# Second layer in a different cyclic order, its start written out, its first buffers loaded during the experts

## What is computed

```
x = x + L0_xattn(layernorm(x), ctx)     # 16 heads
x = x + L0_ffn(layernorm(x))            # routing to 8 experts, 512 places each, token kept or sent
x = x + L1_xattn(layernorm(x), ctx)     # 16 heads, then relu(out @ W1 + b1) @ W2 + b2
x = x + L1_ffn(layernorm(x))            # the cell below, then a layernorm
```

```
for c in range(6):
    q = ew[c,0]*(nodes[in_q] @ We[eq] + be[eq])      # k, v likewise, from other nodes and edges
    nodes[c] = act_w[c]*mha(q, k, v, Wq[c], Wk[c], Wv[c], Wo[c]) + q
```

## Time and profile before

| | |
|---|---|
| profiled execution | 4160.97 us, of which the span of the trace is 4159.2 us |
| median of the three timed runs | 4163.48 us |
| PE busy | 4031.4 us (97% of the span) |
| ACT, DVE, POOL busy | 2628.5 (63%), 2472.9 (59%), 1932.9 (46%) |
| first layer, experts, second layer | 0 to 654, 658 to 897, 897 to 4159 us |
| DMA | mean 31 GB/s over the span |

### The profile page before, as it was taken

The page is one execution under the profiler, slowest core; times in us unless marked ns, Lnnn a source line. Parts: engine busy times, 40 slices in busy tenths (PEclk is TensorE's granted clock), DMA queues, the critical chain, the costliest instruction groups (busy, mean ns, idle before and its releaser), DMA issues.

```text
span 4159.2 us, 100757 instructions
## 1 busy us (share of the span) xinstructions
PE 4031.4 (97%) x38276; PEld 3405.7 (82%) x38276; DVE 2472.9 (59%) x6184; ACT 2628.5 (63%) x11786; POOL 1932.9 (46%) x2011
## 2 busy tenths in 40 slices
PE   7999998988999999999999999999999999999997
PEld 6888876666888888888888888888888888888885
DVE  5777772024566666666666666666666666666553
ACT  6888871214666666666666666666666666666664
POOL 6888982113444444444444444444444444444332
PEclk9999999999999999999999999999999999999999
DMA  3232214430000000000000000000000000000000
GB/s 102 70 98 72 70 45 140 132 116 23 12 14 14 14 17 21 13 14 14 13 13 16 13 13 13 12 12 12 12 12 12 12 20 12 12 12 12 7 4 6
DMA packets 117867, 129.75 MB, mean 31 GB/s; under 512 B 12006, under 2 KB 110676, under 8 KB 117264
## 3 DMA queue, kind: packets, MB, share of 16 engines
q1 hardware_dynamic: 101664, 106.26, 8.0%
q0 software_dynamic: 6144, 8.43, 0.7%
q10 hardware_dynamic: 9584, 8.61, 0.7%
HBM read 89.68 MB, written 41.94 MB: 32 GB/s over the span
## 4 chain that ended last, share of the span: by engine, by line
PE 75%; DVE 1%; ACT 1%; DMA 0%; POOL 0%; issue 0%; ACTq 0%; POOLq 0%; SPq 0%; DVEq 0%
PE c_product L1374 35%; PE c_product L1385 15%; PE c_product L1433 10%; PE c_scores L1423 7%; PE c_product L1456 5%; PE c_product L1444 2%; ACT c_probs L1187 1%; DVE c_qT L1233 1%; PE c_product L1362 1%; PE c_product L1493 0%; DVE c_neg_max L1242 0%; DMA c_probsT<-in_L_ffn_Wk 0%; ACT c_front_probs L1187 0%; POOL c_probs L1135 0%; DMA c_probsT<-in_L_ffn_Wv 0%
## 5 line engine op out<-in xcount | busy, mean ns | idle before, releaser
L1135 POOL TENSOR_TENSOR c_probs<-c_probs,c_row_inv 128x512 f32<-128x512 f32 x768 | 794.2, 1044 | 1525.8 <-DVE c_row_inv L1245 1525.1
L1187 ACT ACTIVATE c_probs<-c_scores,c_neg_max 128x128 f32<-128x128 f32 x3072 | 1086.6, 409 | 606.1 <-DVE c_neg_max L1242 606.1
L1374 PE MATMUL c_product<-c_nodes,cell_w 128*128 128x256 f32 x4352 | 1064.2, 384 | 6.1 <-DVE c_nodes L1233 3.9
L1374 PEld LDWEIGHTS c_product<-c_nodes,cell_w 128*128 128x128 f32 x4352 | 802.6, 190 | 133.1 <-DVE c_nodes L1233 12.8
L1187 ACT ACTIVATION_READ_ACCUMULATOR c_probs<-c_scores,c_neg_max 128x1 f32 x3072 | 762.1, 248 | 0.0
L1242 DVE TENSOR_REDUCE c_neg_max<-c_scores 128x4 f32<-128x512 f32 x1024 | 635.6, 683 | 179.7 <-PE c_scores L1423 179.5
L1193 ACT COPY c_probsT<-c_product 128x512 f32<-128x512 f32 x768 | 416.2, 611 | 237.8 <-PE c_product L1433 235.0
L1187 ACT ACTIVATE c_front_probs<-c_scores,c_neg_max 128x128 f32<-128x128 f32 x1024 | 359.0, 401 | 149.0 <-DVE c_neg_max L1242 149.0
L1385 PE MATMUL c_product<-cell_w,c_nodes 128*128 128x256 f32 x1792 | 432.7, 381 | 1.6 <-DVE c_kT L1233 1.6
L1433 PE MATMUL c_product<-consts_sb,c_probs 128*128 128x128 f32 x3072 | 403.1, 275 | 15.2 <-POOL c_probs L1135 15.0
L420 ACT ACTIVATE a_probs<-a_scores,a_neg_max 128x128 f32<-128x128 f32 x1024 | 361.9, 399 | 82.3 <-DVE a_neg_max L476 81.7
(11 more groups left out here) (167 smaller groups left out, 6679.4 us busy)
## 6 DMA issues: line engine op xcount, KB each, us to landing
e_w<-in_L_ffn_w SPq DMA_DIRECT2D x12, 1024.0 KB, 6.5
a_x<-in_x SPq DMA_DIRECT2D x32, 256.0 KB, 2.9
a_ctxT<-in_ctx_pairsT SPq DMA_DIRECT2D x32, 256.0 KB, 3.1
x<-a_x SPq DMA_DIRECT2D x32, 256.0 KB, 2.2
xn<-a_xn SPq DMA_DIRECT2D x32, 256.0 KB, 2.1
c_routed<-xn SPq DMA_DIRECT2D x32, 256.0 KB, 2.9
c_x<-x SPq DMA_DIRECT2D x32, 256.0 KB, 3.2
c_ctxT<-in_ctx_pairsT SPq DMA_DIRECT2D x32, 256.0 KB, 2.8
```

The source lines that it names most:

```text
L1135: nc.gpsimd.tensor_tensor(e, e, rinv[:, i, r].unsqueeze(2).broadcast_to([P, 4, T]), ALU.mult).then_inc(norm_made, 1)
L1187: a = nc.scalar.activation(probs(n)[:, r, k], S[r][:, k], ACT.Exp, bias=nmax[:, i, r, k:k + 1], accum_out=rsum[:, i, r, k:k + 1])
L1374: i = T_.matmul(m[:, u], w[:, k, u * P:(u + 1) * P], src[:, k], start=n == 0, stop=n == last)
```

## The change

Four edits are made in one.

1. The four order tables are replaced by others. PE's new period has the pairs A2 S0, S3 A5, A0 f.Sb0, A3 S1, A4 S2 and the three A1 f.Sb1 f.Ab0 directly behind one another (A0 f.Sb0 and A4 S2 stood so before). The front part of a job now begins one period earlier (offset -1).
2. The first pieces of each engine are written out in PE_HEAD (99 pieces), DVE_HEAD, ACT_HEAD and POOL_HEAD, with F and B pieces among them; `headed` puts the table ahead and takes its pieces out of the unfolded order.
3. The weights and biases of the second layer, the four ring buffers' first contents and job 0's rows and context are loaded by SP in the experts' block, at experts 4 to 7. Their memory is given out before the experts' phase. The routed rows of expert 0 are waited for by SP before it loads w2 of expert 0.
4. f.Ab0 and f.Ab1 write a buffer of their own (`front_oT`) instead of sharing xT; the stores of finished jobs are issued five jobs later instead of three (STORES_BEHIND), ahead of the context load; POOL zeroes vE and vO behind its first gather.

```
 PE_ORDER = """
-S3:2 T0.1:1 f.Tx:0 f.K:0 V3:2 f.Q:0 A0:1 f.Sb0:0 K1:1 O0:1 T3.0:2 K4:2 T3.1:2 Q1:1 A3:2 f.Tb0.0:0 S1:1
...
+O4:2 f.Ab1:0 Q5:2 f.W1a:0 f.W1b:0 f.Tx:-1 f.W2:0 T2.0:1 S5:2 T2.1:1 V2:1 f.Q:-1 f.Txn:0 V5:2 Q0:0 K0:0 A2:1
...
+def headed(table, order):
+    head = [(t.rpartition(":")[0], int(t.rpartition(":")[2])) for t in table.split()]
+    return head + [x for x in order if x not in head]
...
+            sp.wait_ge(rows_in[0], 16)
             sp.dma_start(w2t[:, 0], tiles(w2[0])).then_inc(w2_in[0], 16)
...
+                if e == 4:
+                    for n, a in (("wk", "L1_xattn_Wk_rows"), ("wq", "L1_xattn_Wq"), ("wv", "L1_xattn_Wv_rows"),
+                                 ("w1", "L1_xattn_W1"), ("w2", "L1_xattn_W2")):
+                        sp.dma_start(early[n][:], tiles(io[a])).then_inc(early[n + "_in"], 16)
...
+                if e == 6:
+                    for n in range(FUSED_FIRST, FUSED_FIRST + len(early["late"])):
+                        fuse_load(sp, io, fused, n, early)
+                if e == E - 1:
+                    sp.dma_start(early["routed"][:], rows_of(scratch["xn1"], 0)).then_inc(early["rows0_in"], 16)
+                    sp.dma_start(early["x"][:, 0], rows_of(scratch["x1"], 0)).then_inc(early["x0_in"], 16)
+                    sp.dma_start(early["ctxT"][:], tiles(io["ctx_pairsT"][0])).then_inc(early["ctx0_in"], 16)
...
-        oF = xT
+        oF = sb("front_oT", [2, W2])
...
-            late_load(act, FUSED_FIRST)
...
             for j in range(2, JOBS):
                 load_rows(j)
+                if j >= STORES_BEHIND:
+                    store(j - STORES_BEHIND)
                 load_context(j)
-                if j >= JOBS_IN_FLIGHT:
-                    store(j - JOBS_IN_FLIGHT)
```

More of the change, by code:

```diff
@@ L895 @@
+S4.e1:1 S4.e2:1 S4.e3:1 f.Tb0^2:-1
 """
 POOL_ORDER = """
[L898 to L910 removed]
@@ L911 @@
-f.Tb0.0:0 B14
-f.Ab0:0 F15 F16 B15
-f.Tb1.0:0 B16 F17
-f.Tb1.1:0 B17
-"""
-LATE_FUSE_DVE_PLACES = """
-start:0 F6^ B6^ F7^
-f.x2:0 B7^
-f.st:0 F8^ B8^
-f.x:0 F9^ B9^ F10^
-f.Tx^:0 B10^
-f.Q^:0 F11^
-f.x2:1 B11^
-f.Sb0.i1:0 F12^
-f.Sb0.i3:0 B12^ F13^ B13^
-f.x:1 F14^ B14^
-f.Sb1.i0:0 F15^
-f.Ab0^:0 F16^
-f.Sb1.i2:0 B15^
-f.Sb1.i3:0 B16^ F17^ B17^
-"""
-def phase_second_layer(nc, io, scratch, keep, cell, cst, out):
+S5.n3:3 S0.n2:1 S0.n3:1 S3.n0:2 S3.n1:2 f.ga:-1 S3.n2:2 f.Sb0.n0:0 S3.n3:2 f.Sb0.n1:0 S1.n2:1 S1.n0:1 S1.n1:1
@@ new lines @@
+f.Tb0.0:1 Q1:0 B15:0 S1:0 K2:0 V1:0 K3:0 f.Tb0.1:1 f.Sb1:1 T1.0:0 T1.1:0 F17:0 A1:0 f.Ab0:1 O1:0 f.Tb1.0:1
+f.Tb1.1:1 Q2:0 f.Ab1:1 S2:0 f.W1a:1 f.W1b:1 f.Tx:2 f.W2:1 V2:0 B16:0 T2.0:0 f.K:2 f.Txn:1 K0:1 Q0:1 T2.1:0
+S0:1 A2:0 O2:0 B17:0 Q3:0 T0.0:1 S3:0 V3:0 f.Q:2 V0:1 T0.1:1 K1:1 f.Sb0:2 A0:1 T3.0:0 O0:1 T3.1:0
+"""
+ACT_HEAD = """
+f.Sb0.e0:0 f.Sb0.e2:0 f.Sb0.e1:0 f.Sb0.e3:0 f.Tb0^1:0 f.Tb0^0:0 f.Tb0^3:0 f.Tb0^2:0 f.Sb1.e2:0 f.Sb1.e0:0
+f.Sb1.e1:0 f.Sb1.e3:0 f.Tb1^0:0 f.Tb1^1:0 f.Tb1^2:0 f.Tb1^3:0 S0.e0:0 S0.e1:0 S0.e2:0 S0.e3:0 T0^0:0 V0^:0
@@ L940, in phase_second_layer @@
+f.Sb0.n0:3 f.Sb0.n1:3 f.Sb0.n2:3 e.rs:0 S1.n2:2 S1.n0:2 S1.n1:2 S1.n3:2 f.Sb0.n3:3 S4.n0:1 S4.n1:1 f.x3b:0
+f.Sb1.n2:3 S4.n3:1 S4.n2:1
+"""
+SECOND_ROWS_BEHIND, SECOND_CONTEXT_BEHIND = 13, 15
+def phase_second_layer(nc, io, scratch, keep, cell, cst, early, out):
     ctx = io["ctx_pairsT"]
@@ L1489, in _ @@
                     c, k, edge = fused[int(n[1:])]
-                    m, we = product(n, j)[:, 0], late[int(n[1:]) % LATE_RING][1]
+                    m, we = product(n, j)[:, 0], late[int(n[1:]) % len(late)][1]
                     for o in range(2):
```

238 lines of the change are left out of this document (140 added, 98 removed).

## The result

The kernel after takes 4099.85 us (median of 4 runs, 4099.14 to 4101.14), the kernel before 4163.52 beside it: a ratio of 0.9849, 95% interval 0.9837 to 0.9861. Two later sets of runs gave 4100.54 and 4100.80. The forecast said 4121, in a range from 4104 to 4142: the sign was right, and the gain of 64 us is half as large again as the 42 that was forecast.

A forecast was written before the change was run, and what follows sets the result against it. PE, busy 97% of the span, was taken as the bound. 23.9 + 6.85 + 10 + 4 - 1 - 1 = 42.8 us off the 4159.2 span, plus 1.8 around it and 2.5 to the median, gave 4121, range 4104 to 4142.

The forecast's parts named there:

- Blocks: PE's order: fewer blocks of strip pieces, 296 instead of 446, save shape changes: 23.9 us, bounds 15 and 26.5.
- the stall behind K0 and A2: In PE's period, S0 waits 0 to 0.1 us on some 29 jobs: a loss of 1 us.
- Start: Second layer's start: with operands loaded during the experts, PE begins with POOL, at about 897.1: 6.85 us saved.
- Head's idle time: PE before 1110 us: 22.15 us idle falls to 12 with the new head; 10 saved, bounds 0 and 22.
- Half clock in the head: Products slowed by the low clock in the head cost 5.8 us; 4 saved, bounds 0 and 6.
- Tail: End of the last jobs: idle time stays, K4 between T3.1 and A3 costs about 1 us; bounds -3 and +4.
- Median against profile: Last step from profiled execution to median of the runs: 2.5 us added, 4118.2 to 4120.7.
- Rival (b): PE's strips: every change of shape costs a full entry, 8.9 us less saved, 4130; chance 0.08.
- (a): Each period stalls, ACT late for f.Ab0 or a writer for its scores: 14 us given back, 4135; chance 0.17.
- (e): Slower: f.Tb0's last copies miss f.Ab0 by over 1.5 us every period; at 2 us a job 4177; chance 0.05.
- (c): Head saves only the gap, bound by job 0's chain, and the clock still falls: 14 less, 4135; chance 0.1.
- Rival (d): Head filled better than seen, 5 us idle left and no half clock: 4111; chance 0.1.

The follow-up runs named there:

- e6: Kernel after with K4 between A3 and S1 on PE in each period, instead of ahead of both: 4106.08 us, ratio 0.9799.
- e5b: Kernel after with O1 between f.Sb1 and f.Ab0 on PE in each period, DVE's evictions swapped alike: 4105.02 us, ratio 0.9857.
- e2: Kernel before with only the early loads of the second layer's first buffers, POOL's clears behind the first gather: 4154.84 us, ratio 0.9983.
- e9: Kernel before with the end of the kernel after's orders put into all four engines' lists: 4180.54 us, ratio 0.9979.
- e5: Kernel after with f.K between S3 and A5 on PE in each period, DVE's evictions not swapped: 4227.30 us, ratio 1.0085.
- e3: Kernel before with O5 of job 30, and its DVE and POOL pieces, moved behind S3 of job 31: 4163.24 us, ratio 1.0005.

## Why the prediction was wrong, step by step

- **Blocks, 23.9 us, and the stall behind K0 and A2, -1: right together, each a little off.** The period fell by 0.78 us, forecast "about 0.8"; over 31 periods that is 24.3, against 22.9 for the two terms. The prices of entering and leaving strips hold, as e6 and e5b bear out. The 2.6 us that A ahead of scores should have given back aren't there: it costs 1.01, as alone. The stall is there, 0.08 us in some 29 periods, so 2.2 us and not 1, near the upper end of the "0 to 0.1" of the forecast. The idle time of the full stretch, 3.1 us against 2.8, doesn't show it.
- **Start, 6.85: right**, 6.9 measured. e2 gains 8.4 with it alone. The experts' first wait, 0: right.
- **Head's idle time, 10: too low.** It is 15.1: 7.1 us stay, not 12. Of my list f.Sb0 (1.2, measured 1.0), the transpositions (2.3, measured 1.9) and S0 (1.0, 1.0) hold, and W1 and W2 nearly (0.6, 0.5). At f.Txn and Q0 0.8 stands instead of 1.8, and T0.0 (1.0) shows no wait at all; of the 4 "in small pieces" some 2 are there, 0.8 of them at job 1's Q0. Where I found no filler PE_HEAD has one.
- **Half clock in the head, 4 with bounds 0 and 6: too low.** 6.2 by windows (7.9 to 1.7). I had counted three places with visibly slow products, 5.8; the low level stood for 23.9 us in windows that show a product at a time between.
- **Tail, a loss of 1 us, with bounds from a gain of 3 to a loss of 4: wrong, and the sign too.** A gain of 6.1 measured, 7.2 of it by idle time, against 1 us more busy time. The forecast said that the place of one job's nodes relative to the next's is the same in both orders. It is the same to a whole node, but not to the piece: the new order spreads K3, T5, A5 and O5 into four waits of node 3. e9 puts that end into the kernel before and gets 6.5. Two more waits, in O0 and O1, went with the order ahead of it. The loss of 1 us for K4 between T3.1 and A3 had no row behind it.
- **Median against profile.** I added 2.5 us, as the kernel before had; the kernel after's median lies 1.3 below its profiled execution.

Summed: PE's idle time fell by 13.9 us more than forecast (5.1 in the head, 0.7 in the full stretch, 8.1 at the end), its busy time by 5.6 more (2.5 of clock, some 3 not told apart). Less 2.1 of a longer first layer and 0.3 outside the span, and with the 3.8 of median and profile, that is the 20.9 us. The failed step is the tail: the one term whose mechanism was wrong, and with 6.1 in its place the forecast is 4114, which still lies 14 above the measured time. The rest are sizes, the head's two terms above all. Rival (b), a drain at every change, is refuted by e6, e5b and the rows; (a) and (e) by the full stretch, whose lists show no wait of PE; (c) by 15.1. Rival (d) comes nearest; by its own terms, 7 us of idle time and 1.8 of clock, it is 4112 and not 4111, and it still had the tail as a loss of 1.

## What to carry to other kernels

The end of a cyclic order is worth a pass of its own: list each wait of the last job and ask which piece of the job before, of those that stand where PE has work anyway, could stand in it. When pieces move on one engine, move their evictions on the next in the same order, and look what these then stand ahead of: e5 and e3 both failed by such a place on DVE, ahead of a bank that PE needs and ahead of the reciprocals that POOL needs. The clock is best read in windows of 2 us, since slow products that stand alone hide part of its price (5.8 us by single products in the head before, 7.9 by windows). A wait of 0.1 us shows in no list; it shows in the distance between starts, laid beside the same pair elsewhere.
